# A vision tower with a mixture of experts: the first four chunks of tokens pass through all experts densely instead of being scattered and gathered

## The reference, cut to what matters

```
logits = x @ gate_w + gate_b;  probs = softmax(logits);  idx = argmax(probs)
pos = (cumsum(one_hot, 0) * one_hot).sum(-1) - 1;  kept = pos < C     # C = 7843 tokens per expert
buf = zeros((E, C, D)).at[idx, pos_safe].set(x, mode='drop')
hmid = relu(einsum('ecd,edf->ecf', buf, w1) + b1)                     # D = 64, F = 256, E = 8
ybuf = einsum('ecf,efd->ecd', hmid, w2) + b2
y_tok = ybuf[idx, pos_g] * (prb * kept)
```

## Time and profile before

| | us |
|---|---|
| median of 3 runs (lowest to highest) | 4369.61 (4355.78 to 4375.41) |
| the profiled execution | 4352.22 |
| its span, from first to last instruction | 4350.4 |
| window attention and gated memory, to | 1579 |
| routing: tables, to | 1646 |
| routing: scatter, to | 2169 |
| experts, to | 2500 |
| image recurrence, to about | 3230 |
| slice attention, to the end | 4350 |

### The profile page before, as it was taken

The page is one execution under the profiler, slowest core; times in us unless marked ns, Lnnn a source line. Parts: engine busy times, 40 slices in busy tenths (PEclk is TensorE's granted clock), DMA queues, the critical chain, the costliest instruction groups (busy, mean ns, idle before and its releaser), DMA issues. The chain is left out here.

```text
span 4350.4 us, 68616 instructions
## 1 busy us (share of the span) xinstructions
PE 3192.8 (73%) x25552; PEld 1809.5 (42%) x25552; DVE 2524.8 (58%) x3049; ACT 2137.7 (49%) x3049; POOL 2570.2 (59%) x1541
## 2 busy tenths in 40 slices
PE   8999996999999940000099946666666899999998
PEld 6777774455555520000034312222221455555556
DVE  7888886988888851000055513333337777777772
ACT  6666675777777720000034435556552444444444
POOL 7777773877788716777600065555506666666661
PEclk9999998999999965555599957877777999999999
DMA  1111111122222121111133323333330122112211
GB/s 42 38 40 40 40 40 57 58 73 86 70 77 75 46 69 38 40 45 35 21 108 109 100 61 100 96 94 99 93 94 21 41 55 55 52 50 56 54 48 41
DMA packets 301346, 267.20 MB, mean 61 GB/s; under 512 B 99368, under 2 KB 229580, under 8 KB 300957
## 3 DMA queue, kind: packets, MB, share of 16 engines
q1 hardware_dynamic: 264718, 228.51, 17.3%
q0 software_dynamic: 25600, 21.10, 2.7%
q10 hardware_dynamic: 10704, 13.20, 0.9%
HBM read 127.66 MB, written 140.20 MB: 62 GB/s over the span
## 5 line engine op out<-in xcount | busy, mean ns | idle before, releaser
L1512 POOL DMA_INDIRECT D_row<-yb,D_idx x400 | 381.9, 955 | 628.3 <-DMA D_prob<-keepp 349.6
L2150 POOL TENSOR_TENSOR E_w<-E_w,E_rs 128x1024 f32<-128x1024 f32 x200 | 380.2, 1901 | 366.8 <-DVE E_rs L2073 366.8
L1241 POOL DMA_INDIRECT xb<-R_row,R_si x400 | 388.9, 972 | 212.4 <-issue 121.5
L1314 PE MATMUL X_px<-X_ident,X_xs 128*128 128x128 f32 x256 | 42.9, 291 | 558.6 <-DMA X_xs<-xb 558.6
L180 POOL TENSOR_TENSOR A_kmask<-A_ksb,A_pack_a 128x3584 f32<-128x3584 f32 x56 | 356.4, 6364 | 152.5 <-ACT A_ksb L327 152.5
L1373 ACT ACTIVATE X_hm<-X_ph,X_b 128x512 f32<-128x512 f32 x128 | 88.0, 688 | 594.6 <-PE X_ph L1326 594.6
L2058 DVE TENSOR_REDUCE E_mx<-E_lg 128x16 f32<-128x1024 f32 x200 | 244.8, 1224 | 220.3 <-PE E_lg L1867 220.1
L1388 DVE COPY X_xt<-X_px 128x512 f32<-128x512 f32 x64 | 43.6, 681 | 530.1 <-PE X_px L1314 530.1
L2144 POOL TENSOR_TENSOR E_hs<-E_w 128x512 f32<-128x512 f32 x200 | 254.7, 1274 | 97.1 <-ACT E_w L2031 97.1
L1879 PE MATMUL E_z<-E_w,E_yk 128*64 128x512 f32 (+1 forms) x800 | 223.7, 632 | 78.1 <-POOL E_w L2150 77.8
L1314 PEld LDWEIGHTS X_px<-X_ident,X_xs 128*128 128x128 f32 x256 | 27.5, 143 | 607.3 <-DMA X_b<-in_e_b 558.8
(11 more groups left out here) (292 smaller groups left out, 8412.6 us busy)
## 6 DMA issues: line engine op xcount, KB each, us to landing
xb<-B_blank SPq DMA_DIRECT2D x64, 256.0 KB, 3.9
X_xs<-xb SPq DMA_DIRECT2D x64, 256.0 KB, 2.8
yb<-X_ys SPq DMA_DIRECT2D x64, 256.0 KB, 2.0
B_x<-h SPq DMA_DIRECT2D x25, 512.0 KB, 4.3
h<-B_hh SPq DMA_DIRECT2D x25, 512.0 KB, 3.7
y<-B_yt SPq DMA_DIRECT2D x25, 512.0 KB, 2.6
R_row<-y SPq DMA_DIRECT2D x25, 512.0 KB, 3.4
A_xg<-in_xw SPq DMA_DIRECT2D x56, 224.0 KB
```

What stands on the lines that cost most here:

```text
L1241: pool.indirect_dma_start(out=xb, out_offset=bass.IndirectOffsetOnAxis(ap=si[:, B * c + b:B * c + b + 1], axis=0), in_=row[c % U][:, D * r ...
L1512: pool.indirect_dma_start(out=row[n % LR][:, k, b], out_offset=None, in_=yb, in_offset=bass.IndirectOffsetOnAxis(ap=idx[:, c, i:i + 1], ax ...
L2150: TT(w3, w3, bc(rs[g % 3][:].unsqueeze(2), [128, 2 * SH, G]), ALU.mult).then_inc(w_done, 1)
```

## The change

Blocks with index below DENSE = 1 in a pair, that is chunks 0 to 3 of every image (512 tokens of each image, 8192 in all), are no longer scattered. Instead `routing` computes for them all eight experts, in 8 blocks of a pair by 512 tokens (S = 64 steps of one block and one expert). A step: a matmul with a 16-row selector spreads the transposed choice to all channels (`mask`), DVE multiplies it with the transposed tokens (`masked`), then come up-projection, relu and down-projection, all eight experts accumulating in one PSUM bank; a correction for the biases of the experts not chosen is added by one matmul (`bias`). At the block's end the sum is multiplied with the weight (spread by `prob`) and added to the hidden state h1, which is loaded and stored back in place by DMAs that ACT issues. This stands beside POOL's scatter, which begins with chunk 4: 336 DMAs. The tiles of the pass lie in the memory of tables no longer needed; `row` has 4 buffers instead of 6. The expert weights come in one packed DMA (`pack_x`) in routing and again in experts.

In `image_recurrence` the first block of each pair (`sparse(n)` false) has no gather, weighting, transpose or addition: x is the hx tile itself. Because of that, its buffer is free only after `add_hidden`, and SP's load for the block three later waits for `h_done` in place of `x_done`. `experts` keeps its 64 blocks. POOL clears 63 semaphores before routing, before it was 40.

```
-def routing(nc, a, lg, y2, xb, gidx, keepp):
+def routing(nc, a, lg, y2, xb, gidx, keepp, h1):
-        N, U = CHUNKS * B, 6
+        N, U = CHUNKS * B, 4
...
+                pe.wait_ge(totc_done, len(cuts))
+                pe.wait_ge(prb_done, 1)
...
+                def mask(s):
+                    i, e = divmod(s, E)
+                    pe.wait_ge(ohc_done, i + 1)
+                    after(pe, xe_done, s - 1)
+                    mm(ob[s % 2], pick[:, 2 * D * e:2 * D * e + 2 * D], oht[i % 2], start=True, stop=True).then_inc(mask_done, 1)
...
+                def up(s):
+                    pe.wait_ge(xe_done, s + 1)
+                    for f in range(2):
+                        if s >= 1:
+                            pe.wait_ge(relu_a, by_act(s - 1, f))
+                            pe.wait_ge(relu_v, by_dve(s - 1, f))
+                        for b in range(2):
+                            last = mm(ph[b][f], w1[HALF[b], s % E, 128 * f:128 * f + 128], xe[s % 3][HALF[b], :],
+                                      start=True, stop=True)
+                        last.then_inc(up_done, 1)
...
+                def down(s):
+                    for f in range(2):
+                        pe.wait_ge(relu_a, by_act(s, f))
+                        pe.wait_ge(relu_v, by_dve(s, f))
+                        for b in range(2):
+                            last = mm(acc[HALF[b], :], w2[:, s % E, f], hm[s % 2][:, b, f], start=False,
+                                      stop=s % E == E - 1 and f == 1, skip_group_check=True)
+                    last.then_inc(down_done, 1)
...
+                for s in range(S + 1):
+                    i, e = divmod(s, E)
+                    if s < S:
+                        up(s)
+                    if s + 2 < S:
+                        mask(s + 2)
+                    if e == 2 and i + 1 < NB:
+                        turn_x(i + 1)
+                    if e == 4 and i + 1 < NB:
+                        turn_oh(i + 1)
+                    if e == 6:
+                        prob(i)
+                    if s >= 1:
+                        if (s - 1) % E == 0:
+                            bias((s - 1) // E)
+                        down(s - 1)
...
+                def masked(s):
...
+                    TT(xe[s % 3], ob[s % 2], xt[i % 2], ALU.mult).then_inc(xe_done, 1)
...
+                def final(i):
...
+                    TT(xo[i % 2], px, yt[i % 2], ALU.mult).then_inc(t_done, 1)
+                    dve.wait_ge(t_done, i + 1)
+                    dve.wait_ge(hx_in[i % 3], 16 * (i // 3 + 1))
+                    TT(xo[i % 2], xo[i % 2], hx[i % 3], ALU.add).then_inc(xo_done, 1)
...
             def _(pool):
                 pool.wait_ge(si_done, 1)
-                for c in range(CHUNKS):
+                first = BT * DENSE
+                for c in range(first, CHUNKS):
...
@@ image_recurrence, sync @@
                 def load(n):
-                    after(sp, x_done, n - LH + 1)
+                    if n >= LH:
+                        if sparse(n - LH):
+                            sp.wait_ge(x_done, before(n - LH) + 1)
+                        else:
+                            sp.wait_ge(h_done, n - LH + 1)
...
@@ image_recurrence, vector @@
                 def weigh(n):
+                    if not sparse(n):
+                        return
...
                 def add_experts(n):
+                    if not sparse(n):
+                        return
```

More of the change, by code:

```diff
@@ L1174, in _, with turned, own, relu @@
                 A(flat(X), flat(X), ACT.Exp).then_inc(exp_done, 1)
+                act.wait_ge(w_in, 32)
+                act.wait_ge(prb_done, 1)
+                def turned(i):
+                    act.wait_ge(turn_done, i + 1)
+                    after(act, xe_done, E * (i - 1))
+                    A(xt[i % 2], px, ACT.Copy).then_inc(xtc_done, 1)
+                def own(i):
+                    act.wait_ge(oht_done, i + 1)
+                    after(act, down_done, E * (i - 1))
+                    A(oht[i % 2], px[0:2 * E, :], ACT.Copy).then_inc(ohc_done, 1)
+                def relu(s, f, b):
+                    act.wait_ge(up_done, 2 * s + f + 1)
+                    after(act, down_done, s - 1)
+                    k = 2 * (s % E) + f
+                    A(hm[s % 2][:, b, f], ph[b][f], ACT.Relu, bias=part["b1"][:, k:k + 1]).then_inc(relu_a, 1)
+                def leave(i):
+                    act.wait_ge(down_done, E * (i + 1))
+                    after(act, t_done, i - 1)
+                    A(yt[i % 2], acc, ACT.Copy).then_inc(yt_done, 1)
+                def hidden(i):
+                    after(act, xo_done, i - 2)
+                    act.dma_start(hx[i % 3], h1[where(i)[0], :, cols(i)]).then_inc(hx_in[i % 3], 16)
+                def keep(i):
+                    act.wait_ge(xo_done, i + 1)
+                    act.dma_start(h1[where(i)[0], :, cols(i)], xo[i % 2]).then_inc(x_out[i % 2], 16)
+                turned(0)
+                own(0)
+                for s in range(S):
+                    i, e = divmod(s, E)
+                    relu(s, 0, 0)
+                    if s % 2:
+                        relu(s, 0, 1)
+                    relu(s, 1, 0)
+                    if e == 0 and i >= 1:
+                        leave(i - 1)
+                    if e == 2 and i + 1 < NB:
+                        turned(i + 1)
+                    if e == 4 and i + 1 < NB:
+                        own(i + 1)
+                    if e == 5 and i >= 1:
+                        keep(i - 1)
+                    if e == 5 and i + 2 < NB:
+                        hidden(i + 2)
+                leave(NB - 1)
+                keep(NB - 1)
             @block.vector
@@ L1202, in _ @@
                 TT(X[:], L[:], by(mx), ALU.subtract).then_inc(sub_done, 1)
+                dve.wait_ge(w_in, 32)
+                TS(rb1[:], part["b1"].rearrange("p (e f) -> p e f", f=2), 0.0, None, ALU.max).then_inc(rb_done, 1)
+                dve.wait_ge(rb_done, 1)
+                for f in range(2):
+                    last = TT(r8[:, :, f], bc(rb1[:, :, f:f + 1], [128, E, 2 * E]),
+                              part["other"].rearrange("p (e k) -> p e k", e=E), ALU.mult)
+                last.then_inc(r8_done, 1)
                 dve.wait_ge(totc_done, len(cuts))
@@ L1282, in _ @@
             def _(sp):
-                with nc.allow_non_contiguous_dma(reason="biases by partition"):
-                    spread(nc, sp, loads[:-1], consts)
+                sp.dma_start(pack[:], a["pack_x"]).then_inc(consts, 16)
                 def load(n):
@@ L1363, in _ @@
                 A = nc.scalar.activation
-                with nc.allow_non_contiguous_dma(reason="biases by partition"):
-                    spread(nc, act, loads[-1:], consts)
                 act.wait_ge(consts, CN)
```

243 lines of the change are left out of this document (197 added, 46 removed).

## The result

| | before | after |
|---|---|---|
| time, median (us) | 4370.87 (4355.78 to 4375.41, 4 runs) | 4558.76 (4554.89 to 4571.01, 4 runs) |
| ratio, 95% interval | | 1.0442 [1.0417, 1.0467], slower |
| profiled execution, span | 4352.22, 4350.4 | 4561.92, 4560.1 |
| last scatter starts | 2155.7 | 2093.3 |
| last store of the dense pass | | 2415.4 |

4290 was predicted. Experts start 250.4 us later, 4.7 us come back in their start and 35 in the recurrence: +210.7, against +209.7 between the two profiled executions (+188 between the medians: the profile of before lies 19 us under the median of this table, the profile of after 3 above its own).

What follows compares the result with a forecast made beforehand. Bounds: POOL's DMA count in the scatter, PE in experts, an ACT-DVE-PE chain in the recurrence. Terms sum to -79.7 us: profiled 4352.2 gives 4272, and with that execution 17 us below the median, 4290 (4268 to 4312).

Steps and rivals of the forecast that it cites:

- part 2: Routing: the dense pass runs hidden beside the scatter, 0 us, with about 75 us of cover.
- part 1: Routing's scatter: 64 of 400 DMAs go at 1.276 us each, -81.7 us.
- Part 9: Recurrence: stalls ending in "remote", 51.1 us of ACT's idle, left as they are, 0 us (-20 to +10).
- Part 3: Routing's scatter: POOL slowed by working beside a busy DVE, +5 us (0 to 9).
- Rival C: Routing: the pass's DVE instructions block POOL's descriptors for their full time, slower, 4412 us; chance 0.03.
- Rival D: Routing: the dense pass runs with PE at 1.2 GHz throughout, slower, about 4530 us; chance 0.02.
- Parts 4 and 5: Stage borders: 23 more semaphores to clear, +1 us; experts start sooner through one packed weight DMA, -3 us (-5 to +1).
- Part 6: Start of the recurrence: the first block needs no gathers, so everything behind stands earlier, -10 us.
- Part 7: Recurrence: 8 of 56 turns lack weighting, transposes and addition, -7 us (-3 to -20).
- Part 8: Recurrence: SP's new wait for `h_done` delays yk's store and DVE's copy, 2.0 x 8 turns, +16 us (+5 to +28).
- rival A: Recurrence gives a good part back: SP's wait costs +28, start and dense turns bring nothing, 4319 us; chance 0.16.
- B: Rival: the recurrence gains more, stalls shrinking with traffic and dense turns bringing 15, 4257 us; chance 0.17.

Runs made afterwards that it cites:

- e1: Changed kernel with GpSimd waiting for the whole dense pass before its first scatter; 4581.8 us, held visit.
- x1: Changed kernel with the 64 gathers of the dense first block put back, into a buffer nobody reads; 4136.8 us, free visit.
- s2: Kernel before plus three independent instruction streams on PE, DVE and ACT beside its 400 scatters, run in a held visit; 4562.9 us.
- s1: Kernel before plus three independent instruction streams on PE, DVE and ACT beside its 400 scatters, run in a free visit; 4191.4 us.
- s3: Kernel before plus the three streams on PE, DVE and ACT, with index bound 0 so nearly no row is written; 4187.1 us, free visit.
- v1: Changed kernel with a bound of 0 on the scatter index, so nearly no row is written; 4162.4 us, free visit.
- v2: Changed kernel with its 336 indirect DMAs writing 32 rows in place of 128; 4102.8 us, free visit.
- p1: Changed kernel with GpSimd waiting after each chunk of 8 scatters until they have landed; 4188.6 us, ratio to before 0.9991, free visit.
- b1: Kernel before with only the experts' weights loaded as one packed DMA; 4358.4 us, ratio 0.9992, held visit.
- a1: Changed kernel run again unaltered as a control; 4572.5 us, ratio to before 1.0473, held visit.
- a2: Changed kernel run a third time, unaltered; 4541.8 us, ratio to before 1.0453, held visit.
- q1: Changed kernel with GpSimd waiting for each chunk of 8 scatters to land and 5 buffers for hidden tokens; 4508.4 us, ratio to before 1.0377, held visit.
- e4: Changed kernel with its 336 scatters as plain DMAs to consecutive rows from GpSimd's own queue; 4157.2 us, held visit.

## Why the prediction was wrong

**The step that failed is part 2**, "The dense pass: hidden, 0 us, with about 75 us of cover". Its length was right: predicted 340 us (1653 to 1993), measured alone 345.5 (e1), beside the scatter in a free visit done by 2001 (x1). Of its terms, the 8 us for a cold clock fit e1, where the granted clock is 0.50 to 0.53 until 1670 us and 1.00 in the 10 us behind it. So was the way to count what is paid without cover: the pass took 2415 - 1653 = 762 us, 340 more than 422, and less the 82 of part 1 that gives 258. What failed is the cover. The step took for granted that engines that share no data run beside each other at the pace that each has alone. In held visits they don't: an engine gets one instruction per 1.40 us beside a scatter without pauses (s2), and of 346 us of work 20 were covered. Experts' first DMA therefore comes 250.4 us later instead of 76 earlier (parts 1, 3 and 4). One of the prediction's own signs of being wrong came with it, PE's last matmul in routing (2413) after GpSimd's last DMA (2093).

**Part 9 had the evidence and set it aside.** The earlier trace rows is one of six rows of its kind: before's list for the recurrence also has

```profile
ACT D_hid L1619 <- remote: 34.8, 14, 9.9
ACT D_sq L1625 <- remote: 26.7, 4, 12.8
DVE D_x L1666 <- remote: 14.5, 4, 4.4
DVE D_yk L1697 <- remote: 12.6, 3, 5.6
ACT D_r L1593 <- remote: 10.2, 3, 5.0
```

Together 149.9 us. In the free visits the same recurrence (s1, s3) has no such row, and takes 596.1 and 593.1 us instead of 754.9. The waits, on two engines whose idle times can overlap, add to about that difference, and the trace of before has none outside the recurrence, the one stage in which engines work beside indirect DMAs. The prediction read 51 of them as noise of unknown origin in a stage that the change hardly touched, and never asked what ends them, though the change set the same company on purpose 340 us long.

**Part 1**: 64 scatters went, and without company each takes 1.277 us (e1). Right.

**Part 3**, +5: in free visits 335 intervals take 429.6 us (x1) against 427.5 undisturbed, +2. Held, 444.3, +17. GpSimd loses little; the others lose. The row that the part was priced from was misread: 333 ns between two gathers were put down to the working DVE, but in s1, with the same recurrence and DVE work, it is 305 ns (121.1 / 397). The 29 ns belong to the held visit. Rival C forecast the right direction (4412), but its mechanism, a DVE that blocks GpSimd, did not occur: DVE was busy 39 us of 100 in x1 and GpSimd kept its 79 scatters. The trace agrees with the Trainium skill's exemption (SBUF — State Buffer, Who interferes with whom). The skill also says, in Runtime: NRT & Kernel Launch, Instruction fetch mechanics, that an engine fetches its next instructions while it executes and that this is mostly hidden. If what is held up is this supply, s2 contradicts "mostly hidden" for held visits. No run shows when a fetch lands; the profiles only list the same sum of instruction DMAs in s1 and s2 (216 packets with 3.54 MB and 118 with 0.97).

**Rival D**: PE at 1.2 GHz throughout. It did not happen: the clock was at 0.50 to 0.53 while PE was mostly idle beside the scatter, and at 1.00 with PE busy (2150 to 2250; x1 beside the scatter).

**Parts 4 and 5**: the start came as described (-3 predicted, 7.4 against 12.1 measured, -4.7). The 23 clears can't be seen in the time: the first scatter starts at 1646.5 to 1652.0 in the traces with them, at 1644.6 to 1650.9 in those without.

**Part 6**, -10: h of turn 0 starts 43.9 us after the `idx` load instead of 56.9, of which the turn behind gives 2 back. Right.

**Part 7**, -7: nothing to be seen. In free visits h of the dense turn follows the one ahead by 10.3 us (v1), in before by 8.7 or 10.4.

**Part 8**, +16: the mechanism happened as described. DVE's copy started 3.75 us after h's end (predicted 2.9 to 4.6), and seven waits make 26.4 us. The net term, 2.0 a turn, looks too small: in free visits h of the turn behind a dense one comes after 14.4 us (v1) where before has 8.4 or 10.1, +4.3 to +6, and the changed recurrence takes 627.5 to 647.4 us there (v2, v1, p1) instead of 593.1 to 596.1. This is rival A's direction. How much of it is this wait alone was not measured in a free visit: x1 has the same seven waits (27.0 us) and loses only some 23. In held ones five buffers brought 10 us, within the spread.

**Why then -35 in the recurrence**, with a cost where I saw one? First, -35 is one pair of profiles: the held recurrence of before took 754.9 and 755.2 us (before, b1), that of the changed kernel 719.9, 750.5 and 694.8 (after, a1, a2), so -4 to -60. What is left may come from 64 of 400 gathers gone, which take with them part of the 160 us that holding costs there. x1, meant to show this, ran in a free visit, so this is argued from the two signs (shorter when held, longer when free) and not shown. The +210.7 adds up with the right total, but the part of it from the recurrence is no prediction that came true.

**In a free visit** the changed kernel itself was not run. p1 is it plus 33 us of pauses at 4188.6, v1 is it with fewer writes at 4162.4, x1 is it with 64 gathers more at 4136.8. An estimate from these is 4137 to 4162 against 4181 to 4183: faster by half to one per cent. The 80 us predicted would not have come there either, since the recurrence is longer.

**The chances**: those of the prediction add to 0.93 for faster (forecast, A and B) and 0.05 for slower (C and D), not to 0.94 and 0.04. The result fell on the side that got the 0.05, by a mechanism that none of the five rivals names.

**What stays open**: what differs between held and free visits; whether GpSimd's making of indirect descriptors or the scattered writes hold the others up (v1, v2 and s3 all fell in free visits); and whether it is really the supply of instructions. For that speak the stores that run out first, the common beat, no need of semaphores, and the recurrence of before, in which PE goes on at 103 matmuls in 60 us after GpSimd's wait of 10.3 us. Against it speaks q1, where pauses of 1.9 us did not refill them. No version that computes everything beats before in a held visit; b1 equals it.

## What to carry to other kernels

Idle engines beside a stream of indirect DMAs need not be free capacity; here they were in free visits and were not in held ones. Before moving work there, look in the trace for a stretch in which an engine already works beside such DMAs, and count the waits there that no semaphore ends. Waits named "remote" or "issue" on several engines at once hint at a shared cause, and are to be priced like any other wait. Time the kernel before again with every comparison: here it differed by 4% between visits, and the effect to be explained was there only in one kind.

## What the runs showed of the hardware

- In a held visit, with indirect DMAs issued from GpSimd every 1.28 us, PE, ACT and DVE each fell to one instruction per 1.40 us, after 43 to 108 instructions at full pace (s2). Plain DMAs from the same queue every 0.53 us left them alone (e4, also held).
- On the same chips, in other visits, nothing of this (s1, x1): the kernel before 4181 to 4183 us instead of 4348 to 4371.
- An indirect DMA of 32 rows costs GpSimd 872 ns in the mean, one of 128 rows 976 (v2, v1): by these two sizes nearly all of it is a fixed price.
